# Masked cross-attention stage: penalties for the row maximum added by VectorE instead of TensorE, and scaled by GpSimd

## The reference, cut to what matters

```python
energy = jnp.einsum('bhqd,bhkd->bhqk', q, k) * scale          # [16, 16, 112, 375]
energy = jnp.where(mask == 0, neg_inf, energy)                # mask: [16, 1, 112, 375] int32
energy = jnp.where(key_padding_mask[:, None, None, :] == 0, neg_inf, energy)   # [16, 375] int32
attention = jax.nn.softmax(energy, axis=-1)
out = jnp.einsum('bhqk,bhkd->bhqd', attention, v)
```

## Time and profile before

| | |
|---|---|
| median of 3 runs | 3426.89 us (3418.62 to 3431.49) |
| profiled execution | 3436.66 us |
| its span in the trace | 3434.9 us |
| TensorE busy in the span | 78% |
| VectorE busy in the span | 57% |
| ScalarE, GpSimd busy in the span | 38%, 27% |
| masked cross stage in the trace | from about 2560 to 2850 us |

### The profile page before, as it was taken

One profiled execution on the slowest core, in us unless ns is written; L12 is line 12 of the kernel. 1 busy time (PEld: TensorE's weight loads), 2 busy tenths in 40 slices (PEclk: granted clock), 3 DMA queues, 4 the chain that ended last, 5 costly groups with the idle time before them and its releaser, 6 DMA issues. The chain is left out here.

```text
span 3434.9 us, 58873 instructions
## 1 busy us (share of the span) xinstructions
PE 2681.5 (78%) x21336; PEld 2089.6 (61%) x21336; DVE 1970.1 (57%) x3596; ACT 1318.6 (38%) x2568; POOL 936.0 (27%) x795
## 2 busy tenths in 40 slices
PE   7997687958979998585786937876758994599993
PEld 7996466946756665362565624544436773588883
DVE  4555665147753223496665157788756553376674
ACT  4444455234551112354455113333333442355551
POOL 3433100020002222203001023354440002677774
PEclk9998799988989999797788968988879996799997
DMA  7888784357830000854872010000057842455552
GB/s 220 238 237 221 145 152 104 136 129 135 149 134 0 1 0 22 132 66 99 147 134 60 0 74 0 1 0 0 1 106 132 147 86 87 163 192 190 207 185 81
DMA packets 193509, 370.65 MB, mean 108 GB/s; under 512 B 23152, under 2 KB 152816, under 8 KB 179872
## 3 DMA queue, kind: packets, MB, share of 16 engines
q1 hardware_dynamic: 182512, 286.12, 38.4%
q0 software_dynamic: 10800, 81.84, 6.4%
HBM read 271.42 MB, written 96.01 MB: 107 GB/s over the span
## 5 line engine op out<-in xcount | busy, mean ns | idle before, releaser
L934 DVE TENSOR_REDUCE arena<-ps 112x2 f32<-112x750 f32 x512 | 469.3, 935 | 266.2 <-PE ps L819 179.4
L918 ACT ACTIVATE arena<-ps 125x448 f32<-125x448 f32 x768 | 410.1, 545 | 464.5 <-PE ps L837 457.8
L470 POOL TENSOR_SCALAR ln_tmp<-ln_tmp 112x16 f32<-112x16 f32 x11 | 2.9, 261 | 1442.2 <-DVE ln_tmp L438 1442.2
L819 PE MATMUL ps<-wreg,arena 96*112 96x375 bf16 x768 | 229.8, 366 | 114.8 <-DMA arena<-values 94.2
L2331 PE MATMUL ps<-moe_x_r,moe_w_r 128*128 128x256 f32 x2016 | 254.8, 287 | 25.4 <-DVE arena L2449 24.0
L2331 PEld LDWEIGHTS ps<-moe_x_r,moe_w_r 128*128 128x128 f32 x2016 | 247.2, 193 | 30.0 <-issue 27.2
L837 PEld LDWEIGHTS ps<-arena,wreg 98*125 98x125 bf16 x2304 | 220.0, 146 | 66.1 <-issue 28.2
L837 PE MATMUL ps<-arena,wreg 98*125 98x112 bf16 x2304 | 241.7, 232 | 4.0 <-ACT arena L918 3.2
L2261 POOL TENSOR_TENSOR moe_w_r<-wreg,moe_w_r 128x512 fp32r<-128x512 f32 x160 | 220.3, 1400 | 35.8 <-ACT moe_w_r L2359 33.6
L1935 POOL TENSOR_TENSOR arena<-arena 112x1024 f32<-112x1024 f32 x64 | 156.5, 2453 | 227.9 <-DVE arena L2049 161.4
L492 PE MATMUL ps<-ident,xn 112*128 112x112 f32 x320 | 72.5, 384 | 184.6 <-DVE xn L451 139.8
(11 more groups left out here) (300 smaller groups left out, 5761.6 us busy)
## 6 DMA issues: line engine op xcount, KB each, us to landing
key_parts<-arena SPq DMA_DIRECT2D x128, 281.2 KB, 4.1
wreg<-key_parts SPq DMA_DIRECT2D x48, 562.5 KB
arena<-query_parts SPq DMA_DIRECT2D x108, 224.0 KB, 8.8
values<-arena SPq DMA_DIRECT2D x64, 357.0 KB
arena<-values SPq DMA_DIRECT2D x64, 357.0 KB
wreg<-key_parts SPq DMA_DIRECT2D x48, 375.0 KB
query_parts<-arena SPq DMA_DIRECT2D x48, 336.0 KB, 2.5
wreg<-in_e_w SPq DMA_DIRECT2D x16, 704.0 KB, 5.2
```

The source lines that it names most:

```text
L819: mm = pe.matmul(ps[0:T, 2 * (p % 2) + e, 0:S2], queries(b)[0:SROWS, hd, :], keys[r][0:SROWS, hd, :], start=True, stop=not masked)
L918: act.activation(probs[k % PROBS], ps[0:KN, 4 + k % 2, 0:GT], ACT.Exp, scale=scale).then_inc(at_probs, 1)
L934: dve.tensor_reduce(negmax[r % 2][:, 2 * p:2 * p + 2], ps[0:T, 2 * (p % 2):2 * (p % 2) + 2, 0:S2], AX.X, ALU.max, negate=True).then_inc(at ...
```

## The change

The matmuls L822 that add the penalties per head are gone. In their place `reduce_pair` takes two instructions of the form `tensor_tensor_reduce`, one for each head: it adds the tile `pen` (SBUF, bf16) to the scores in PSUM, writes the sum back over them, and gives the row maximum. The sign is turned in `clamp`. The 12 matmuls per batch that add the penalties to the score tiles stay, but with a diagonal of 1 (`unit16`), so the penalties must be scaled beforehand: VectorE leaves 0, 1 or 2 as f32 in `pad_in`, and GpSimd multiplies by -1e30 into `pen` (`weighty`). `at_pen` is now raised by GpSimd.

```diff
-        neg16 = sb("neg16", [T, GB, T], BF16)
+        unit16 = sb("unit16", [T, GB, T], BF16)
...
+                def weighty(b, r):
+
+                    at_least(pool, at_pen, p0 + b)
+                    pool.wait_ge(at_pen0, 2 * (p0 + b + 1))
+                    pool.tensor_scalar(pen[r], pad_in[r].bitcast(F32), NEG, 0.0, ALU.mult, ALU.add).then_inc(at_pen, 1)
+
+                if masked:
+                    pool.wait_ge(const_made, ones_made)
+                    for b in range(B):
+                        weighty(b, b % RING)
+
...
                         mm = pe.matmul(ps[0:T, 2 * (p % 2) + e, 0:S2], queries(b)[0:SROWS, hd, :], keys[r][0:SROWS, hd, :],
-                                       start=True, stop=not masked)
-                        if masked:
-                            mm = pe.matmul(ps[0:T, 2 * (p % 2) + e, 0:S2], neg16[:, 0, :], pen[r], start=False, stop=True)
+                                       start=True, stop=True)
                     mm.then_inc(at_pair, 1)
...
                     if masked:
-                        pe.matmul(ps[0:KN, bank, 0:GT], pen[r][:, c * KN:(c + 1) * KN], neg16[:, :, :], start=True, stop=False)
+                        pe.matmul(ps[0:KN, bank, 0:GT], pen[r][:, c * KN:(c + 1) * KN], unit16[:, :, :], start=True, stop=False)
...
                     dve.wait_ge(at_pair, k + 1)
-                    dve.tensor_reduce(negmax[r % 2][:, 2 * p:2 * p + 2], ps[0:T, 2 * (p % 2):2 * (p % 2) + 2, 0:S2], AX.X, ALU.max,
-                                      negate=True).then_inc(at_max, 1)
+                    if masked:
+                        dve.wait_ge(at_pen, p0 + b + 1)
+                        for e in range(2):
+                            bank = ps[0:T, 2 * (p % 2) + e, 0:S2]
+                            mm = dve.tensor_tensor_reduce(bank, bank, pen[r], 1.0, 3 * NEG, ALU.add, ALU.max,
+                                                          negmax[r % 2][:, 2 * p + e:2 * p + e + 1])
+                        mm.then_inc(at_max, 1)
...
+                    if masked:
+                        dve.tensor_scalar(negmax_c[r % 2], negmax[r % 2], -1.0, 0.1 * -NEG, ALU.mult, ALU.min).then_inc(at_clamped, 1)
...
-                    dve.wait_ge(at_pen0, p0 + b + 1)
-                    dve.scalar_tensor_tensor(pen[r], pad_in[r], 0, mask_in[r].bitcast(F32), ALU.is_equal, ALU.add).then_inc(at_pen, 1)
+                    dve.wait_ge(at_pen0, 2 * (p0 + b) + 1)
+                    dve.scalar_tensor_tensor(pad_in[r].bitcast(F32), pad_in[r], 0, mask_in[r].bitcast(F32), ALU.is_equal, ALU.add).then_inc(at_pen0, 1)
```

More of the change, by code:

```diff
@@ L196, in start_gpsimd @@
             pool.memset(ident16[:, :], 0.0).then_inc(const_made, 1)
-            pool.memset(neg16[:, :, :], 0.0).then_inc(const_made, 1)
+            pool.memset(unit16[:, :, :], 0.0).then_inc(const_made, 1)
             pool.memset(nought[:, :], 0.0).then_inc(const_made, 1)
@@ L205, in start_gpsimd @@
                                pattern=[[-1, T]], channel_multiplier=1)
-            pool.affine_select(out=neg16[:, :, :], in_=neg16[:, :, :], compare_op=ALU.not_equal, fill=NEG, base=0,
+            pool.affine_select(out=unit16[:, :, :], in_=unit16[:, :, :], compare_op=ALU.not_equal, fill=1.0, base=0,
                                pattern=[[0, GB], [-1, T]], channel_multiplier=1)
@@ L933, in reduce_pair @@
                     dve.wait_ge(at_pair, k + 1)
-                    dve.tensor_reduce(negmax[r % 2][:, 2 * p:2 * p + 2], ps[0:T, 2 * (p % 2):2 * (p % 2) + 2, 0:S2], AX.X, ALU.max,
-                                      negate=True).then_inc(at_max, 1)
+                    if masked:
[5 more added lines that the diff above has]
+                        mm.then_inc(at_max, 1)
+                    else:
+                        dve.tensor_reduce(negmax[r % 2][:, 2 * p:2 * p + 2], ps[0:T, 2 * (p % 2):2 * (p % 2) + 2, 0:S2], AX.X, ALU.max,
+                                          negate=True).then_inc(at_max, 1)
                 def clamp(b, r):
                     dve.wait_ge(at_max, (n0 + b + 1) * PAIRS)
-                    dve.tensor_scalar(negmax_c[r % 2], negmax[r % 2], 0.1 * -NEG, None, ALU.min).then_inc(at_clamped, 1)
+                    if masked:
+                        dve.tensor_scalar(negmax_c[r % 2], negmax[r % 2], -1.0, 0.1 * -NEG, ALU.mult, ALU.min).then_inc(at_clamped, 1)
+                    else:
+                        dve.tensor_scalar(negmax_c[r % 2], negmax[r % 2], 0.1 * -NEG, None, ALU.min).then_inc(at_clamped, 1)
                 def split_rows(b, r):
```

## The result

The changed kernel takes 3417.96 us (median of 20 runs, 3398.38 to 3431.56), the kernel before, run beside it, 3433.88 (20 runs, 3415.28 to 3444.34). The ratio is 0.9950, with a 95% interval of 0.9935 to 0.9965: some 17 us are gained, between 12 and 22, just at the 0.5% under which the prediction held that no change can be told. The forecast gain, 14.1 us, lies in that interval.

The account below looks back on a forecast made before the run. TensorE sets the step, with the round through VectorE only 0.25 us longer than its work; the changed round sets it next. Terms 12.0 + 2.6 + 4.0 - 1.4 - 3.1 = 14.1 us gained from 3426.89 give 3413 us, range 3398 to 3431.

Parts of the forecast that it names:

- the round through VectorE and GpSimd: Masked stage, pair 0 through last reduction, penalties and GpSimd to the next pair 0: 14.06 us against 15.55.
- P: VectorE's time per pair for both heads' combined instructions: 1.15 us taken, 1.04 lower end, 1.4 upper end.
- the penalty of P - 1.05: Reductions of pairs 6 and 7: when P exceeds 1.05, the last begins later by the excess, 0.1 us in the round.
- D: GpSimd's scaling of the penalties, 112x375: 0.6 us taken, 0.55 worked out, upper end 1.0 to 1.2.
- Plain rounds: Eight masked-stage rounds without query loads, each 1.5 us shorter: 12.0 us gained.
- Query steps: Steps 4 with 5 and 8 with 9, which also load queries: about 2 us gained each pair, 4.0 together.
- Start: Masked stage from first reduction to first score tile: a loss of 1.4 us.
- First step: First masked step at granted clock 0.50 for 8.8 us, plus a wait for GpSimd: a loss of 3.1 us.
- Every VectorE instruction runs to its end: Rival on the combined instructions: P is 1.4, gain 5.6 us, 3421 us; chance 0.17 together with the clock rival.
- Two cycles per element: Rival on the combined instruction: P is 1.85, VectorE sets the step, 34 us lost, 3461 us; chance 0.12.
- GpSimd is not waited for: Rival on the scaled penalties: TensorE's 12.66 us rules the step, 26.6 us gained, 3400 us; chance 0.12.
- The clock falls behind each wait: Rival on TensorE's wait before pair 0: costs 1.56 us a step, no gain, 3427; 0.17 with the run-to-end rival.

Follow-up runs that it names:

- a_pool_alone: Changed kernel with the pairs' penalty matmuls and old reduction kept, so only GpSimd's scaling is new; 3453.61 us in one run, rounds of 16.22.
- b_no_pool: Changed kernel without GpSimd's part: VectorE scales the penalties itself in two instructions; 3415.73 us, ratio 0.9938 to the kernel before.
- e_matmuls_kept: Changed kernel with each matmul of a pair issued twice in all masked batches; 3466.57 us in one run, stage 301.79.
- c_early: Changed kernel with VectorE's two penalty instructions ahead of the last pair's reduction instead of behind it; 3414.42 us, ratio 0.9923 to the kernel before.
- n_after_again: The changed kernel itself, unaltered, timed and profiled once more; 3416.67 us, ratio 0.9947 to the kernel before.
- run d: Changed kernel with a second GpSimd instruction over the same elements ahead of the scaling; stage 278.04 us, undisturbed rounds 14.37.
- f: Changed kernel with each pair matmul issued twice in the masked stage's first two batches only; stage 274.03 us.
- run l: c_early with a 112-row matmul ahead of each pair matmul in the first two masked batches; 3412.09 us, ratio 0.9926 to the kernel before.
- m: Kernel before the change, with the two penalty instructions moved ahead of the last pair's reduction; 3429.89 us in one run, stage 286.70.
- g: Changed kernel with loads of query groups 2 and 3 fetching one head of 16; stage 259.53 us.
- j: c_early with the values loaded ahead of the queries in steps 4 and 8; 3416.04 us, ratio 0.9932 to the kernel before.

## Why the prediction was right

**The mechanism.** The step is set by the round through VectorE and GpSimd, not by TensorE's load, as forecast. a_pool_alone and b_no_pool price GpSimd's link from both sides (0.68 each), e_matmuls_kept the matmuls (2.5 a round), and c_early shows what is left when the last reduction no longer stands in the chain (12.56, where the prediction had 12.66 for TensorE alone). The round was forecast as 15.55 less 2.64 for the matmuls plus 1.15 for the longer chain; e measures the matmuls at 2.54 (16.32 less 13.78) and the chain at 0.77 (16.32 less 15.55).

**The sizes.** The forecast round of 14.06 came out at 13.78: P was 0.98 to 1.01, not 1.15, so the penalty of P - 1.05 did not arise either, and D was 0.52, not 0.6. Idle before pair 0 is then 1.05 instead of 1.4, VectorE's load 10.77 instead of 11.6 us a step. I had worked out P = 1.04 and D = 0.55 from the rows and then taken more for safety; the rows alone would have been better. Term by term:

- Plain rounds, from pair 0 to pair 0: 13.1 us, forecast 12.0. Eight times 15.55 - 13.78 would be 14.2; step 6 (14.99 by its key loads) and the first ones (14.04, 13.93) are longer.
- Query steps, 4 with 5 and 8 with 9: 68.75 us before, 63.84 after, a gain of 4.9, forecast 4.0. The values of the first of them reached TensorE 18.1 us behind the start of step 4 (key load at 2641.42, pair 0 at 2659.49), where I had 18.7; in n_after_again it is 19.0 and the gain 4.1.
- From pair 0 of step 13 to the end 2.6, forecast 2.6.
- Start, first reduction to first score tile: 16.87 to 16.70, a gain of 0.2 where I had a loss of 1.4. This is 14P, with P near 1.0.
- First step, first score tile to pair 0 of step 1: 13.65 to 14.75, a loss of 1.1 where I had 3.1. The clock did start at 0.50, but rose after 6 us (2593.5) where I had taken 8.8 from the earlier trace rows.
- Masks' arrival, memset to first reduction: 21.19 to 19.91, 1.3 us that no step of mine has. Over the 14 profiled executions it took 19.5 to 21.2; I take it as the spread of one profile.

These sum to 20.9. Of the 6.8 us above the forecast, about 3.8 come from the sizes of P and D (2.2 in plain rounds, 1.6 in the start), 2.0 from the first step, 1.3 from the masks and 0.9 from the query steps; the long step 6 and the first steps take 1.1 off. n_after_again, with 267.76, is within 0.2 us of the first profile. So in the stage the change brought half as much again as forecast. That the 17 us of the whole kernel lie nearer to 14.1 than the stage's 20.9 is no merit of the forecast: the change touches nothing outside the stage, and the difference of 3.7 us lies within the spread of the times.

**The rivals.** *Every VectorE instruction runs to its end* falls by the timeline above. The accumulator's read, which depends on the sum ahead of it, starts at 2701.44, before that sum's end (2700.97 + 0.56 = 2701.53), and the next sum starts with it. The Trainium skill, VectorE: DVE Perf Modes, section "The DRAIN you can't avoid", has the next instruction wait until the pipe is empty; by that rule P would be 1.4, and the trace shows 0.98. The same section adds that an instruction which is not held back starts earlier, and that is what the trace agrees with here; the prediction had left this out. The combined instruction's read of the accumulator, 140 ns, costs no time of its own here. *Two cycles per element* falls by the 574 ns of the group. *GpSimd is not waited for* falls by runs a and b. *The clock falls behind each wait* was the closest: it does not occur at 1.05 us and does in every second round at 1.65 (run d). That is in part luck: the prediction let the wait be 1.4 us, and no kernel here has plain rounds with a wait between 1.32 and 1.65. With D at the prediction's upper end of 1.0 to 1.2 the wait would have been about that of run d, whose stage gained 10.4 us and not 20.9.

**My reason for the cold start was wrong.** The prediction lets the first step stay at the 1.2 GHz level "with half of the matmuls gone". The level came true and the reason did not, so the level was luck as far as this reason goes. Runs e and f put the same number of matmuls back and the clock stayed at 0.50 for longer; run l put 112-row ones back and it rose early. So the number of matmuls is not the reason. That the 112 rows are it rests on four kernels that warmed early (before, a, l, m), all with such matmuls among the pairs, and eight that did not (after, b, c, d, e, f, g, j), without them; no run varied the rows alone with all else equal, and the penalty matmuls differ in their data too. In all eight the clock rose 3.5 to 7.5 us behind the first score tile, and the score tiles bring 112-row matmuls again (L843). But such matmuls are not needed: in the unmasked stage of the earlier trace rows the clock rose some 8 us behind the first score tile, and that tile has none (the small f32 ones of 112 rows that turn the maxima stand in every start):

```profile
388.66 0.62 PE L837 MATMUL ps<-arena,wreg 98*125 98x112 bf16 x4
```

So what raised the clock is not shown. Nor is it why 1.43 us of idling dropped it in run l and 1.24 in run m, while 1.44 did not before and 1.25 did not in run a. A start of the changed kernel that keeps the clock was not found.

**Not settled.** The spread of the stage's start over the profiled executions, and the 1.2 us more of step 6, have no cause shown here. The same holds for step 5 of m_before_early, whose pair 0 had its values only 21.7 us behind the start of step 4, against 19.0 before. Masks loaded a step ahead, which could start the penalties earlier still, were not tried.

## What to carry to other kernels

Before removing work from the busiest engine, walk the round: from one instruction that waits, through the other engines, back to the same one in the next iteration. Here 2.6 us of matmuls were removed and 1.8 gained, since the chain behind the last pair took over; putting the instruction on which the next step waits one place earlier in its engine's order, with no change in work, brought 1.2 more. Then look at what such a faster step runs into: the three steps with extra loads took 46 to 48 us in all the kernels with short rounds, and so took part of that gain back. A single change was worth 0.68 or 1.22 us in each plain round and much less than 12 times that in the stage.

## What I had not expected of the hardware

- Matmuls with 96 rows, without a gap for 10.85 us (run f), did not raise the granted clock from 0.50; starts with 112-row ones among them (before, a, l, m) had 1.00 within 5 to 7 us of the first reduction. Whether the rows are the reason is not shown.
- Idle times of 1.24, 1.43, 1.65 and 2.25 us were followed by a granted clock of 0.50 to 0.61, while others of 1.25, 1.44 and 1.66 were not. At 1.05 us it never fell in a plain step.
- The combined VectorE instruction reads PSUM and SBUF and writes PSUM at 574 ns for 375 columns; two follow each other after 0.47 to 0.51 us, with the read of the maximum hidden.
- GpSimd's scaling with two operations took 521 ns for 375 columns, 1.39 ns a column. In the earlier trace rows two operations took 0.94 ns a column (1685 ns for 1792) and one operation 2.65 (4747 ns); each of these is a single instruction.
